# Values token-major in three sixteen-head attentions: exponentials become the stationary operand on TensorE

## The reference, cut to what matters

```python
Q = split_heads(x1 @ Wq + bq, SQ)          # 16 heads of 8
K = split_heads(x2 @ Wk + bk, SK)
V = split_heads(x2 @ Wv + bv, SK)
scores = jnp.einsum('bhqd,bhkd->bhqk', Q, K) / jnp.sqrt(8)
attn = jax.nn.softmax(scores, axis=-1)
ctx = jnp.einsum('bhqk,bhkd->bhqd', attn, V)
return ctx @ Wo + bo
```

## Time and profile before

| what | value |
|---|---|
| time, median of 3 | 1361.57 us (1360.91 to 1361.68) |
| time of the profiled execution | 1361.15 us, of that 1359.4 us span |
| mean granted TensorE clock of the span | 0.901 |
| TensorE matmul busy | 1061.9 us (78%) |
| VectorE busy | 988.6 us (73%) |
| ScalarE busy | 624.9 us (46%) |
| GpSimd busy | 339.9 us (25%) |

### The profile page before, as it was taken

How to read it: one execution, slowest core, us unless ns; L and a number is a source line. 1 busy time by engine, 2 the same in 40 slices (tenths; PEclk the granted TensorE clock), 3 DMA queues, 4 the chain that set the end, 5 groups by cost and what they waited for, 6 DMA issues and landing times.

```text
span 1359.4 us, 21524 instructions
## 1 busy us (share of the span) xinstructions
PE 1061.9 (78%) x7235; PEld 685.3 (50%) x7235; DVE 988.6 (73%) x2359; ACT 624.9 (46%) x972; POOL 339.9 (25%) x350
## 2 busy tenths in 40 slices
PE   2766780067996998799669888888878969999998
PEld 1544430064553775454326666566654536566665
DVE  4687669977786566577689788788567875666665
ACT  2211356735763334665266555555447633333332
POOL 0121000001220001444198767677201210000000
PEclk9888796578998999899859888888999998999999
DMA  7000000001000000000000000000000000000000
GB/s 264 0 1 0 0 0 0 0 1 58 2 2 1 1 1 0 1 2 1 1 1 1 2 1 0 1 0 0 1 1 2 1 1 1 16 8 8 8 8 16
DMA packets 7797, 14.12 MB, mean 10 GB/s; under 512 B 800, under 2 KB 5024, under 8 KB 7328
## 3 DMA queue, kind: packets, MB, share of 16 engines
q1 hardware_dynamic: 7712, 13.05, 2.9%
HBM read 10.95 MB, written 2.10 MB: 10 GB/s over the span
## 4 chain that ended last, share of the span: by engine, by line
PE 44%; DVE 37%; issue 11%; ACT 6%; DVEq 1%; SPq 1%; DMA 0%; POOL 0%; ACTq 0%
DVE big L1127 6%; DVE big L1122 6%; PE psum L1997 4%; PE psum L919 4%; PE psum L2000 4%; PE psum L2011 4%; PE psum L1692 3%; DVE big L1903 2%; PE psum L1484 2%; DVE tmp L1868 2%; PE psum L1437 2%; PE psum L1446 2%; PE psum L247 2%; ACT psum L1760 2%; DVE amax L1247 2%
## 5 line engine op out<-in xcount | busy, mean ns | idle before, releaser
L1122 DVE TENSOR_REDUCE big<-psum 128x16 f32<-128x1024 f32 x96 | 114.4, 1221 | 74.7 <-PE psum L873 38.7
L1817 POOL TENSOR_TENSOR big<-big 128x512 f32<-128x512 f32 x128 | 134.7, 1087 | 20.7 <-ACT big L1740 20.7
L2047 ACT ACTIVATE big<-psum 128x512 f32<-128x512 f32 x80 | 47.9, 598 | 143.3 <-PE psum L1997 143.2
L1760 ACT ACTIVATE psum<-big,tmp 128x512 f32<-128x512 f32 x128 | 85.0, 687 | 42.3 <-DVE big L1903 38.4
L1903 DVE SCALAR_TENSOR_TENSOR big<-big,tmp,psum 128x512 f32<-128x512 f32 x128 | 90.4, 743 | 4.7 <-ACT psum L1760 1.8
L790 POOL TENSOR_TENSOR big<-big,w_const 128x256 f32<-128x256 f32 x48 | 34.8, 726 | 233.3 <-PE psum L919 219.3
L2100 DVE TENSOR_TENSOR big<-big,psum 128x512 f32<-128x512 f32 x80 | 54.4, 687 | 53.1 <-PE psum L2000 52.5
L1827 POOL TENSOR_TENSOR big<-big 128x1024 f32<-128x1024 f32 x32 | 75.4, 2367 | 70.4 <-DVE big L1903 70.4
L1127 DVE RECIPROCAL big<-psum 128x256 f32<-128x256 f32 x48 | 84.0, 1749 | 11.8 <-PE psum L919 11.8
L2011 PEld LDWEIGHTS psum<-tmp,big 128*128 128x128 f32 x512 | 66.7, 191 | 40.1 <-issue 36.4
L1028 ACT ACTIVATE big<-psum 128x1024 f32<-128x1024 f32 x64 | 62.0, 1021 | 51.5 <-PE psum L903 51.5
(11 more groups left out here) (252 smaller groups left out, 2484.2 us busy)
## 6 DMA issues: line engine op xcount, KB each, us to landing
out<-X SPq DMA_DIRECT2D x8, 256.0 KB, 2.3
tmp<-in_pack_f SPq DMA_DIRECT2D x1, 1924.0 KB, 7.5
w_f<-in_pack_f SPq DMA_DIRECT2D x1, 1280.0 KB, 12.3
ctxd<-in_ctxd SPq DMA_DIRECT2D x1, 1024.0 KB, 6.4
tmp<-in_pack_once SPq DMA_DIRECT2D x1, 960.0 KB, 8.6
w_a<-in_pack_a SPq DMA_DIRECT2D x3, 256.0 KB, 12.0
w_f<-in_pack_f SPq DMA_DIRECT2D x1, 576.0 KB, 9.5
w_const<-in_pack_const SPq DMA_DIRECT2D x1, 560.0 KB, 3.9
```

The source lines that it names most:

```text
L1122: dve.tensor_reduce(nm, psum[:, 1 + 2 * t:3 + 2 * t, :].rearrange("p c (r l k) -> p (c r) l k", r=2, k=SK), AX.X, ALU.max, negate=True).th ...
L1760: act.activation(bank(EX_BANK + h % 2), ssum[t][:, h * 512:(h + 1) * 512], ACT.Exp, bias=shift2[:, t * NH2 + h:t * NH2 + h + 1]).then_inc( ...
L1817: ins = pool.tensor_tensor(ssum[t][:, h * 512:(h + 1) * 512].rearrange("p (i j) -> p i j", i=ROWS2), st[:, 0, h, 0:ROWS2].unsqueeze(2).to_ ...
```

## The change

PV is turned round. The exponentials, 128 keys of two heads by 128 tokens, are the stationary operand; what streams is one block of 18 columns: for each of two heads eight columns of values and one column of ones, all of them zero on the other head's keys. So one product gives values and denominators of 128 tokens, and 8 products make PV(b, t) for tokens t. The values' block is made once for all batches by ScalarE in the prologue (two activations for each of four value products, in place of one), the ones by GpSimd once; `weights` on GpSimd goes.

The result is token-major: VectorE takes the reciprocal of 32 columns and multiplies 256. A new step TO(b) on TensorE transposes it, and ScalarE copies it (take_out) as the input of O. TO uses the free half of the bank of NM, so TO(b-2) waits until ScalarE has taken NM(b+1), and NM(b+1) waits until take_out(b-3) is done. O comes one round later, and the loop has two rounds more.

```diff
-                self.V2 = a.take(B * P).rearrange("p (b n) -> p b n", b=B)
-                self.vw = [a.take(256) for _ in range(2)]
+                self.vw = a.take(B * 144).rearrange("p (b c e n) -> p b c e n", b=B, c=8, e=2)
-                self.rz = a.take(256)
+                self.ow = [a.take(256) for _ in range(2)]
+                self.rz = [a.take(32) for _ in range(2)]
...
+            pool.tensor_copy(L.vw[:, :, :, :, 8], W["kmask64"].unsqueeze(1).to_broadcast([P, 8 * B, 2])
+                             .rearrange("p (b c) e -> p b c e", b=B)).then_inc(hs("ones"), 1)
...
-                    weights(2 * g)
-                    weights(2 * g + 1)
                     rows(g)
...
             def V(i):
                 if i:
-                    pe.wait_ge(hs("v"), hat(s, "v") + i)
+                    pe.wait_ge(hs("v"), hat(s, "v") + 2 * i)
...
+                if b >= 4:
+                    pe.wait_ge(hs("oT"), hat(s, "oT") + b - 3)
                 for t in range(2):
                     ins = pe.transpose(bank(5)[:, t * P:(t + 1) * P], L.nm[b % 2][:, t * P:(t + 1) * P], ident)
...
-            def PV(b, which):
-                if which == 0:
-                    pe.wait_ge(hs("kv"), hat(s, "kv") + b + 1)
+            def PV(b, t):
+                if t == 0:
                     pe.wait_ge(hs("pt"), hat(s, "pt") + 2 * b + 2)
                     if b == 0:
                         pe.wait_ge(hs("k"), hat(s, "k") + 8)
+                        pe.wait_ge(hs("ones"), 1 + HSUB.index(s))
                     else:
-                        pe.wait_ge(hs("oT"), hat(s, "oT") + b)
-                for e in range(2):
-                    for r in range(4):
-                        w = W["vmask8"][:, 32 * e:32 * e + 32] if which else \
-                            L.vw[b % 2][:, 64 * r + 32 * e:64 * r + 32 * e + 32]
-                        ins = pe.matmul(bank(6)[32 * r:32 * r + 32, 256 * which:256 * which + 256], w,
-                                        L.pt[b % 2][:, (2 * r + e) * 256:(2 * r + e + 1) * 256],
-                                        start=(e == 0), stop=(e == 1))
-                if which:
+                        pe.wait_ge(hs("ow"), hat(s, "ow") + b)
+                for c in range(8):
+                    ins = pe.matmul(bank(6)[:, 144 * t + 18 * c:144 * t + 18 * c + 18],
+                                    L.pt[b % 2][:, c * 256 + t * P:c * 256 + (t + 1) * P],
+                                    L.vw[:, b, c].rearrange("p e n -> p (e n)"), start=True, stop=True)
+                if t:
                     ins.then_inc(hs("pv"), 1)
+
+            def TO(b):
+                pe.wait_ge(hs("ow"), hat(s, "ow") + b + 1)
+                pe.wait_ge(hs("nmT"), hat(s, "nmT") + min(b + 4, B))
+                if b:
+                    pe.wait_ge(hs("oT"), hat(s, "oT") + b)
+                for t in range(2):
+                    ins = pe.transpose(bank(5)[:, 256 + t * P:256 + (t + 1) * P], L.ow[b % 2][:, t * P:(t + 1) * P], ident)
+                ins.then_inc(hs("to"), 1)
...
-            for b in range(B + 2):
+            for b in range(B + 4):
                 if b < B:
                     ST(b)
                 if 1 <= b <= B:
                     PV(b - 1, 0)
                 if b + 2 < B:
                     MX(b + 2, 0)
+                if 1 <= b <= B:
+                    PV(b - 1, 1)
+                if b + 2 < B:
+                    MX(b + 2, 1)
+                if b + L.ahead < B:
+                    Q(b + L.ahead)
+                if 3 <= b < B + 3:
+                    O(b - 3)
                 if b + 1 < B:
                     NM(b + 1)
-                if b + L.ahead < B:
-                    Q(b + L.ahead)
-                if b + 2 < B:
-                    MX(b + 2, 1)
-                if 1 <= b <= B:
-                    PV(b - 1, 1)
-                if b >= 2:
-                    O(b - 2)
+                if 2 <= b < B + 2:
+                    TO(b - 2)
                 turn_ahead(b)
...
-                act.activation(L.V2[:, 4 * i:4 * i + 4, :].rearrange("p b n -> p (b n)"), bank(5), ACT.Copy)\
-                    .then_inc(hs("v"), 1)
+                for e in range(2):
+                    act.activation(L.vw[:, 4 * i:4 * i + 4, :, e, 0:8],
+                                   bank(5).rearrange("p (b c e n) -> p b c e n", b=4, c=8, e=2)[:, :, :, e, :], ACT.Copy,
+                                   scale=W["kmask64"][:, e:e + 1]).then_inc(hs("v"), 1)
...
+            def take_out(b):
+                act.wait_ge(hs("to"), hat(s, "to") + b + 1)
+                if b >= 2:
+                    act.wait_ge(hs("o_ps"), hat(s, "o_ps") + b - 1)
+                act.activation(L.oT[b % 2], bank(5)[:, 256:512], ACT.Copy).then_inc(hs("oT"), 1)
...
-            for b in range(B):
+            for b in range(B + 2):
+                if b >= B:
+                    take_out(b - 2)
+                    continue
                 exp(b, 0)
                 exp(b, 1)
                 if b + 1 < B:
                     takeN(b + 1)
+                if b >= 2:
+                    take_out(b - 2)
                 norm_half(b)
...
                 dve.wait_ge(hs("pv"), hat(s, "pv") + b + 1)
-                dve.reciprocal(L.rz, bank(6)[:, 256:512]).then_inc(hs("rz"), 1)
+                both = bank(6)[:, 0:288].rearrange("p (h n) -> p h n", n=9)
+                dve.reciprocal(L.rz[b % 2], both[:, :, 8]).then_inc(hs("rz"), 1)
                 dve.wait_ge(hs("rz"), hat(s, "rz") + b + 1)
                 if b >= 2:
-                    dve.wait_ge(hs("o_ps"), hat(s, "o_ps") + b - 1)
-                dve.tensor_tensor(L.oT[b % 2], bank(6)[:, 0:256], L.rz, ALU.mult).then_inc(hs("oT"), 1)
+                    dve.wait_ge(hs("to"), hat(s, "to") + b - 1)
+                dve.tensor_tensor(L.ow[b % 2].rearrange("p (h n) -> p h n", n=8), both[:, :, 0:8],
+                                  L.rz[b % 2].unsqueeze(2).to_broadcast([P, 32, 8]), ALU.mult).then_inc(hs("ow"), 1)
```

More of the change, by code:

```diff
@@ L722, in build @@
         HSUB = ("a1", "a2", "a3")
-        PER = dict(k_ps=1, v_ps=4, k=8, kb=2, ka=2, v=4, zero=2, mask=0, kv=B, q_ps=B, qe=0, qT=B, q16=B, mx_ps=2 * B,
-                   mx=2 * B, nm_ps=B, nmT=B, st_ps=B, pt=2 * B, pv=B, rz=B, oT=B, o_ps=B, r=0, prep=0)
+        PER = dict(k_ps=1, v_ps=4, k=8, kb=2, ka=2, v=8, zero=2, mask=0, kv=0, q_ps=B, qe=0, qT=B, q16=B, mx_ps=2 * B,
+                   mx=2 * B, nm_ps=B, nmT=B, st_ps=B, pt=2 * B, pv=B, rz=B, ow=B, to=B, oT=B, o_ps=B, r=0, prep=0)
         PRIMED = dict(mx=2, nmT=1, pt=2, pv=4, oT=1, o_ps=2)
@@ L784, in rows @@
                     .then_inc(sem(s, "biased"), 1)
-            def weights(b):
-                pool.wait_ge(hs("v"), hat(s, "v") + b // 4 + 1)
-                if b >= 2:
[L789 to L794, removed]
             def rotate(b):
@@ L807, in heads_pool @@
                 rotate(1)
-                weights(0)
                 rotate(2)
-                weights(1)
                 rotate(3)
@@ L815, in heads_pool @@
                         rotate(b + 4)
-                    if b + 2 < B:
-                        weights(b + 2)
                     if b % 2 and b // 2 + 1 < N_GROUPS:
@@ L953, in heads_pe @@
             MX(1, 0)
-            pe.wait_ge(hs("v"), hat(s, "v") + 4)
+            pe.wait_ge(hs("v"), hat(s, "v") + 8)
             NM(0)
@@ L1155, in heads_dve @@
                     norm(b - 1)
-                if b >= 2 and b % 2:
-                    res((b - 3) // 2)
+                if b >= 4 and b % 2 == 0:
+                    res((b - 4) // 2)
             stats_done(dve, s, nxt)
```

## The result

| what | before | after |
|---|---|---|
| median of the runs | 1361.24 us (4 runs, 1359.58 to 1361.68) | 1717.38 us (4 runs, 1714.24 to 1726.72) |
| ratio | 1 | 1.263, 95% interval 1.258 to 1.268 |
| span of the profiled execution | 1359.4 us | 1712.3 us |
| mean granted clock of the span | 0.901 | 0.764 |

The change costs 356 us. The forecast was 1482 (range 1415 to 1540): the sign was right, the size was off by a factor of three, and the time lies far above the range.

The account below looks back on a forecast made before the run. Bound: a loop of VectorE's norm and TensorE's first product, TensorE nearly a second bound. Twelve rounds +31.2 and +9.1 around them make +40.3 a stage; three stages, +121 us on 1361.15, forecast 1482, range 1415 to 1540.

Parts of the forecast that it names:

- the sum: Slots and waits of a1's rounds added up: +31.2 us over twelve rounds, +9.1 around them, +40.3 a stage.
- the clock falls: Rival: gaps and load stretches lower TensorE's clock to a mean of 0.9, 38 us on top, 1521; chance 0.14.
- PV half: TensorE's turned product for one t: 16 loads of 128 columns at 0.111 us each, 1.78 us.
- norm on VectorE: Reciprocal of 32 columns (0.35 us) plus the product of 256 (0.43): from 2.19 to about 0.8 us.
- round of a1 without T: Rounds 3, 5, 7, 9: 3.91 + 4.37 = 8.28 us, with MX waiting 0.55 for the exponentials.
- T after TO: T begins 1.87 us after TO, once ScalarE has taken TO and done norm_half; 1.59 of it wait, six times a stage.
- round of a1 with T: Rounds 2, 4, 6, 8, 10: 1.87 + 0.53 + 1.3 + 1.78 + 4.37 = 9.85 us, the exponentials in time.
- twelve rounds of a1, PV of round 2 to that of round 14: Steady part of a1: 105.2 us against 74.0 before, +31.2.
- The loop through norm: PV waits for the previous batch's norm, the reductions for the MX behind PV; 6.17 us a round, cut by the change.
- Hidden waits: Rival: ScalarE's takes fit in elsewhere, so TensorE's work alone sets the round, 7.09 or 7.62 us; 1421, chance 0.14.
- Columns set the price: Rival: loads hide, a PV half costs 0.24 us; 1385 with waits (chance 0.03), 1313 without (0.03).
- the two rules: Skill's prices for PV: issue gap by streamed columns, 0.8 us at the floor; weight load by columns / 1.2, 3.4 us.

Follow-up runs that it names:

- run 1: Changed kernel with each PV product streaming its 18 columns seven times over (126), same loads, order and waits; 1514.62 us, ratio 1.113 to before.
- run 4: Kernel before with only the reciprocal cut to 32 columns, repeated over eight (values differ); 1339.85 us, ratio 0.985 to before.
- run 5: Changed kernel with 126 columns; NM, Q and MX(b+2, 1) ahead of PV(., 1), TO and O last, take_out behind takeQ; 1423.83 us, ratio 1.046.
- run 2: Changed kernel, still 18 columns, with NM and Q ahead of PV(., 1), TO and O last, take_out behind takeQ; 1559.3 us, ratio 1.145 to before.
- run 3: Changed kernel with both the 126 streamed columns of run 1 and the mended order of run 2; 1446.07 us, ratio 1.062 to before.
- run 9: Changed kernel with the order of run 5, exponentials and values in bfloat16, and 18 columns streamed once; 1339.99 us, ratio 0.987 to before.

## Why the prediction was wrong

**What failed.** The step is the clock: the sum takes every slot of TensorE at the upper level, and the rival "the clock falls" was given 0.14 and priced at a mean of 0.9, 38 us. The clock measured 0.50 in nearly all of a1's rounds (0.54 in the mean), and the part of its loss that goes away with more streaming is 203 us (change against run 1, in which nothing but the streaming differs). The 0.9 came from no row. Against a fall stood only that TensorE had kept 0.97 when busy half the time, in 420 to 430. But that stretch was busy with products that stream 128 and 256 columns, and it kept its clock through waits of 1.78 and 1.69 us; a stretch of loads with 18 columns behind each is counted as busy by the profile just the same. The busy share of before could not carry over to another mix, and a lower clock should have been priced at 0.50, where eight loads took 2.04 us and TensorE's 7.1 us of a round would double. After, a round of a1 without T at that clock took 14.19 us (norms at 375.65 and 389.84). (The reading that TensorE "had been idle for several us" before that row is loose too: its waits there were 1.93, 1.65 and 0.69 us, with short work between them.)

**What held, by its steps.** With the clock held the terms come out as follows.

| term | forecast | measured |
|---|---|---|
| PV half | 1.78 us | 1.90 (18 columns), 1.98 (126) |
| norm on VectorE | 0.8 | 0.77 |
| round of a1 without T | 8.28 | 8.19 (after, at full clock), 8.12 (run 1) |
| T after TO | 1.87 | 2.37 |
| round of a1 with T | 9.85 | 12.3, once 10.74 (run 1) |
| twelve rounds of a1, PV of round 2 to that of round 14 | 105.2 | 116.1 (run 1), 174.6 (after) |
| whole kernel | 1482 | 1515 (run 1), 1717 (after) |

The round with T is 2.5 us longer than the forecast. 0.5 of it is a missed wait: T(g) also waits until takeQ has read the bank it writes, and takeQ now comes behind norm_half. 2 x 0.2 are PV's halves, in part by the added columns. The rest, 1.6, is the fall of the clock behind the wait, as the one round without it took 10.74 and not 12.34; 1.35 of that is the first PV half (3.33 against 1.98). The twelve rounds took 462.29 - 346.18 = 116.1 in run 1, 10.9 more than forecast, and three times that is the 33 us between 1482 and 1515. (The intervals of the table above grew by 41.3, 42.3 and 43.0 us in a1, a2 and a3, so a1 may stand for all.) Most of this second miss is the clock again, four falls of 1.6 in a1; the missed wait is 5 x 0.5.

The round without T came out right in part by chance. The forecast has 0.55 us in it in which MX waits for the exponentials. There is none: in run 1 MX starts at 388.68, with no idle before it. Longer PV halves (1.98 and 1.99 for 1.78) took most of its place.

**The rivals.** Hidden waits: refuted; taking them away by another order is worth 69 us with 126 columns. Columns set the price: refuted, 0.119 a load with 18 columns and 0.124 with 126. Of the two rules the weights' was the right one for float32.

**Where the gain went.** The loop through norm was real, but run 4 shows that cutting it alone gives 22 us, since TensorE's slots and half an exponential are the next bound, 0.4 us below in a round without T and nothing in one with it. The turned PV puts 1.8 us a round on just that engine; run 5, with no wait and no lost clock, shows what is left of that price behind the gain, +63 us. The order adds 22 + 69 = 91 to reach run 1 (1446 - 1424 and 1515 - 1446), the narrow stream 203 more: 63 + 91 + 203 = 357, the 356 that were measured. These are the steps along one path. The 91 have the short falls of the clock behind T in them, and by way of run 2 the order is 158 and the stream 113, since the two strengthen each other.

What stays open: why the changed kernel had a stretch at full clock from 409 us and nowhere else in a1's rounds, why one wait in six left the clock alone, and whether float32 as such has a share. The runs show that streaming and waits both move the clock; by what rule, they do not.

## What to carry to other kernels

Before turning a product round so that the long operand becomes stationary, count the loads by 128 columns each and put them against the slack of TensorE, not against the engine that is relieved. When the new mix has long stretches of loads with few streamed columns, price it also at the lower clock, whatever the busy share says, and try a few repeated columns: streaming more made this kernel 203 us faster. Where the rounding is allowed, the narrower type did more: a PV half went from 1.90 us to 0.22. A step that joins two in-order engines (here NM, take, TO, take) belongs early in the round, with the takes that others need ahead of it.

## What the runs showed of the hardware that was not expected

TensorE at 100% busy by the profile, without a wait, was granted a mean of 0.67 of its clock over 20 us (run 2, 360 to 380), and 1.00 with the same loads and seven times the columns (run 3). A bfloat16 load of 128 columns with its 18 streamed columns took 0.027 us where a float32 one took 0.119 (run 9 and the changed kernel). And repeating the streamed columns from 18 to 126 cost almost nothing in time at the same clock: 1.90 against 1.98 us for sixteen.
